# First stage of a graph and attention kernel: the load of x on two queues, roots and masks on GpSimd, the keys' first layer norm on ScalarE

## The chip, the cores and the metric

The kernel runs on one core of a Trainium2 chip. The core has TensorE (PE, matmuls), VectorE (DVE), ScalarE (ACT), GpSimd (POOL) and SyncE (SP), which work in parallel, each through its own instructions in order, and meet only at semaphores; 16 DMA engines move data. The metric is the device time of one execution in microseconds, lower is better. A profile comes from one execution of its own.

## The reference

The input is a graph of 6250 nodes with 256 features each and 106250 edges. With `xn` the layer norm of `x`:

```python
x = x + gnn(xn, edges) + mixer(xn)   # mixer: 4 layers of linear attention and feed-forward
x = x + experts(_layernorm(x))       # one of 32 experts for each node
# gnn: sums edge_attr by src with segment_sum, two dense layers
# mixer layer: h = layernorm(x, ln1_g, ln1_b); q = softmax(h Wq) over features,
#   k = softmax(h Wk) over the nodes; x += attention; x += gelu(layernorm(x) W1 + b1) W2 + b2
```

Only the first stage matters here. It does three things: it sorts the edges by their node's *kind* (the tile in which the node lies, 50 kinds), so that the sums by node can be made tile by tile later; it computes mean and variance of every row of `x`, and from them two layer norms (the first, `xn`, and the norm of `xn`, with which layer 0 begins); and it computes keys and queries of layer 0 for all nodes.

## The kernel before

Nodes lie as 50 tiles of 125 rows (`P = 125`, `TILES = 50`), taken in 25 pairs, the `GROUPS`. All of `x` stays in SBUF in `res`. Each engine has a program of its own, written out by hand; the order in each program is the order of its work.

*Load.* `block_.sync` issues the source indices `src_i`, then `res` in two halves of 25 tiles (3125 KB each, semaphores `X_LOADED[0]` and `[1]`), then the small vectors (`colrows`), then the mixer's weights.

*Sort.* VectorE makes, for each of 50 kinds, a 0/1 mask of 125x850 edges (`kind_mask`), and TensorE counts with it (`count_edges`). `first_ranks` turns the counts into starts. Then come the ranks: for kind `b`, TensorE computes with the mask the position of each edge (`rank_edges`, two halves in two banks), and VectorE writes it where the mask holds (`kind_place`, two predicated copies) and makes the mask of kind `b + 4`, as four mask buffers rotate. Eight kinds are placed ahead of the moments (`RANKS_EARLY = 8`); the other 42 go two to a key step, up to step 20.

*Statistics.* `moments` runs `bn_stats` on each tile, `variance` combines them, and `newton` computes the inverse root with 11 small operations, once for the first norm (`xst`) and once for the second (`kst`).

*Key phase.* 25 key steps, `key_step(t)` on each engine. VectorE: the shift by the maximum (`ek`), `key_normalise` (`xh`), the second placement of the step before, running maximum (`kmax`), softmax of the queries (`qstat`, `qd`, `qn`), the first placement of this step. TensorE: keys and queries of the pair before (`wqk`, 16 products), the first ranks, four transposes of `xh`, the weighing of an older pair (`xh,ek`), the second ranks. ScalarE: exponentials, a copy of the keys (`kr`), the scaled transposes (`h`), and the normalised `res`. GpSimd sums exponentials (`es`) and is otherwise free. Every fourth step or so computes a block's maximum (`MAX_AT`), the one behind it a block's sum (`SUM_AT`). When all kinds are placed, the positions go to the DMAs that scatter the edges; these run through the next three layers, on GpSimd.

TensorE transposes the small vectors (line 2125) after its early ranks, and ScalarE copies them to `cols`, which both it and VectorE await before the key phase.

## Time and profile before

| | us |
|---|---|
| median of 3 runs | 3080.54 |
| lowest, highest | 3072.39, 3084.48 |
| the profiled execution's own time | 3077.36 |
| its span in the profile | 3075.2 |

| engine | busy us | share of the span |
|---|---|---|
| TensorE, matmul | 2715.3 | 88% |
| VectorE | 2125.2 | 69% |
| GpSimd | 1723.8 | 56% |
| ScalarE | 1528.0 | 50% |

Line numbers (L1175) are those of the kernel before. A releaser behind an arrow is what the engine waited for. A matmul's end is modelled, so a group's time can overlap the next one's start. `PEclk` is the share of full speed that TensorE was granted, 0.50 or 1.00 at any moment, and a mean over a stretch. The DMA share is the mean over the 16 DMA engines.

### The profile page before, as it was taken

Reading aid. Unit: us, or ns where it says so; the run is one execution under the profiler, and the core shown is the slowest. Engines: PE = TensorE matmul, PEld = TensorE weight load, DVE = VectorE, ACT = ScalarE, POOL = GpSimd, SP = SyncE. Lnnn points to the kernel's source line nnn. Section 1 sums busy time; section 2 is a strip of 40 time slices with the busy share of each in tenths; the row PEclk is TensorE's granted clock in tenths of the full one; section 3 lists DMA queues with packets and bytes.
Section 4 is the critical chain, followed back from the end, with each engine's and each line's share of the span. In section 5 each row is a group of like instructions: output and inputs, shape, how many; then the busy total and the mean of one; then the engine's idle time right before and its main releaser. Section 6 shows DMA issues by size and latency. Waiting matters only on the chain.

```text
span 3075.2 us, 56118 instructions
## 1 busy us (share of the span) xinstructions
PE 2715.3 (88%) x18842; PEld 2482.9 (81%) x18842; DVE 2125.2 (69%) x4836; ACT 1528.0 (50%) x2947; POOL 1723.8 (56%) x1611
## 2 busy tenths in 40 slices
PE   4888899999979999997999999788888888992597
PEld 2666799999978999996889999688888888992465
DVE  8887567677756666675567767688888886893144
ACT  0333366666635566662565666344444445771254
POOL 0011178777758888885888885154454553224455
PEclk7898899999989999998999999799999998996688
DMA  3000223323232223223223221233323322201332
GB/s 119 24 27 25 82 50 68 68 61 64 54 93 66 63 68 65 59 62 95 64 59 68 65 64 43 64 108 84 87 81 87 82 81 60 59 25 50 85 100 76
DMA packets 255488, 207.87 MB, mean 68 GB/s; under 512 B 165433, under 2 KB 194314, under 8 KB 255205
## 3 DMA queue, kind: packets, MB, share of 16 engines
q1 hardware_dynamic: 197606, 162.55, 19.7%
q0 software_dynamic: 57600, 41.75, 7.0%
q8 instruction: 154, 2.52, 0.4%
q14 instruction: 128, 1.05, 0.1%
HBM read 136.93 MB, written 70.16 MB: 67 GB/s over the span
## 4 chain that ended last, share of the span: by engine, by line
PE 18%; POOL 13%; issue 8%; DVE 7%; DMA 4%; ACT 2%; DVEq 1%; SPq 0%; POOLq 0%; ACTq 0%
PE bank L375 16%; POOL edges_sorted L725 8%; DMA nodes_out<-orow,oidx 3%; POOL tokens_sorted L790 2%; DVE xh L1266 2%; PE bank L1808 1%; DVE hidh_lo L1302 1%; DMA staging<-in_edge_attr 1%; POOL r L703 1%; DVE oh L1494 1%; POOL ehl L742 1%; DVE bn L1257 1%; ACT hidh_hi L837 1%; ACT ehl L913 1%; ACT hid L831 0%
## 5 line engine op out<-in xcount | busy, mean ns | idle before, releaser
L725 POOL DMA_INDIRECT edges_sorted<-staging,pos_i x850 | 1058.2, 1245 | 254.2 <-issue 230.8
L831 ACT ACTIVATE hid<-bank,b1p 128x250 f32<-128x250 f32 x800 | 331.9, 466 | 388.0 <-PE bank L375 385.8
L375 PE MATMUL bank<-h_hi,w_hi 128*128 128x250 f32 x1600 | 482.7, 302 | 19.7 <-DVE h_lo L1286 19.7
L1302 DVE TENSOR_TENSOR hidh_lo<-hid,hidh_hi 128x500 fp32r<-128x500 f32 x400 | 296.9, 742 | 272.6 <-ACT hidh_hi L837 265.1
L375 PE MATMUL bank<-w_hi,hidh_hi 128*125 128x256 f32 x1600 | 468.1, 293 | 0.0
L375 PE MATMUL bank<-h_hi,w_lo 128*128 128x250 f32 x1600 | 451.1, 282 | 0.0
L375 PE MATMUL bank<-w_hi,hidh_lo 128*125 128x256 f32 x1600 | 450.9, 282 | 0.0
L375 PE MATMUL bank<-w_lo,hidh_hi 128*125 128x256 f32 x1600 | 449.8, 281 | 0.0
L375 PE MATMUL bank<-h_lo,w_hi 128*128 128x250 f32 x1600 | 448.0, 280 | 0.0
L375 PE MATMUL bank<-wqk,h 128*125 128x256 f32 x1600 | 380.6, 392 | 0.6 <-ACT mbc L882 0.6
L375 PEld LDWEIGHTS bank<-wqk,h 128*125 128x125 f32 x1600 | 306.3, 195 | 47.4 <-issue 1.2
L375 PEld LDWEIGHTS bank<-h_hi,w_hi 128*128 128x128 f32 x1600 | 307.0, 192 | 28.0 <-DVE h_lo L1286 24.2
L837 ACT CAST hidh_hi<-hid 128x500 fp32r<-128x500 f32 x400 | 243.8, 609 | 145.9 <-PE bank L375 139.6
L375 PEld LDWEIGHTS bank<-h_lo,w_hi 128*128 128x128 f32 x1600 | 308.4, 193 | 1.9
L375 PEld LDWEIGHTS bank<-h_hi,w_lo 128*128 128x128 f32 x1600 | 305.0, 191 | 0.0
L375 PEld LDWEIGHTS bank<-w_hi,hidh_hi 128*125 128x125 f32 x1600 | 298.6, 187 | 2.0
L375 PEld LDWEIGHTS bank<-w_lo,hidh_hi 128*125 128x125 f32 x1600 | 297.8, 186 | 2.2
L375 PEld LDWEIGHTS bank<-w_hi,hidh_lo 128*125 128x125 f32 x1600 | 297.3, 186 | 0.0
L703 POOL TENSOR_TENSOR r<-ve,minus_half 125x2 f32<-125x2 f32 x175 | 140.6, 804 | 271.5 <-DVE ve L1262 268.3
L1494 DVE TENSOR_TENSOR oh<-iota_node,kb 128x1000 fp32r<-128x1000 f32 x153 | 228.8, 1496 | 59.6 <-POOL kb L737 59.6
L1266 DVE TENSOR_SCALAR xh<-res,mv,r 125x256 f32<-125x256 f32 x350 | 159.0, 496 | 155.7 <-POOL r L703 155.7
L375 PE MATMUL bank<-ehl,oh 128*125 128x130 f32 x1224 | 164.4, 278 | 65.0 <-DVE agg L1482 65.0
(289 smaller groups left out, 5754.5 us busy)
## 6 DMA issues: line engine op xcount, KB each, us to landing
staging<-edges_sorted SPq DMA_DIRECT2D x103, 260.0 KB, 2.7
staging<-in_edge_attr SPq DMA_DIRECT2D x50, 531.2 KB
queries<-qn SPq DMA_DIRECT2D x100, 250.0 KB
qin<-queries SPq DMA_DIRECT2D x100, 250.0 KB
edges_sorted<-staging,pos_i POOLq DMA_INDIRECT x850, 3.7
rows_in<-edges_sorted SPq DMA_DIRECT2D x50, 260.0 KB, 2.7
yin<-tokens_sorted SPq DMA_DIRECT2D x81, 127.0 KB
raw<-in_L_mix_W SPq DMA_DIRECT2D x8, 1024.0 KB, 6.3
```

What stands on the lines that cost most here:

```text
L375: return nc.tensor.matmul(o, left, right, start=start, stop=stop, skip_group_check=True)
L703: nc.gpsimd.tensor_tensor(o[:, :], ve[:, :], minus_half[:, :], ALU.pow).then_inc(done, 1)
L725: nc.gpsimd.indirect_dma_start(out=edges_sorted, out_offset=bass.IndirectOffsetOnAxis(ap=pos_i[:, i:i + 1], axis=0), in_=stage[:, slot, j, ...
L742: nc.gpsimd.tensor_tensor(ehl[n % 4][:, :, EA + 2:2 * EA + 2], rows_in[n % RIN][:, :, 0:EA], f32(ehl[n % 4][:, :, 0:EA]), ALU.subtract).th ...
L790: nc.gpsimd.indirect_dma_start(out=tokens_sorted, out_offset=bass.IndirectOffsetOnAxis(ap=fpos_i[:, t:t + 1], axis=0), in_=res[:, t, :], i ...
L831: a = nc.scalar.activation(hid[c % 2][:, j, :], chunks(PH[c % 2])[:, j, :], ACT.Gelu, bias=b1p[:, 2 * c + j:2 * c + j + 1])
L837: nc.scalar.copy(hidh[c % 2][0][:, :, :], hid[c % 2][:, :, :]).then_inc(f_hi, 1)
L913: nc.scalar.copy(ehl[n % 4][:, :, 0:EA], rows_in[n % RIN][:, :, 0:EA]).then_inc(s_hi, 1)
L1257: step_(nc.vector.bn_stats(st[:, j, :], res_row(PAIR * g + j)))
L1266: a = nc.vector.tensor_scalar(o[:, j, :], res_row(PAIR * g + j), mv[:, j, 0:1], r[:, j:j + 1], ALU.subtract, ALU.mult)
L1302: nc.vector.tensor_tensor(hidh[c % 2][1][:, :, :], hid[c % 2][:, :, :], f32(hidh[c % 2][0][:, :, :]), ALU.subtract).then_inc(f_lo, 1)
L1494: nc.vector.tensor_tensor(oh[n % 4][:, :, :], iota_node[:, :].unsqueeze(1).to_broadcast((128, SEGR, P)), kb[:, n % 4, :].unsqueeze(2).to_b ...
```

## The change

- The second half of `x` is issued by ScalarE instead of SyncE, as ScalarE's first instruction.
- The two roots are powers (exponent -0.5) on GpSimd over 125x50; VectorE hands over the variance, and waits for the result. `newton` is gone.
- The early ranks move behind the moments, in two halves of four, each beside one of GpSimd's roots.
- The masks of kinds 12 to 49 are made by GpSimd, two a step from step 1 on, one step ahead of their use; VectorE no longer makes any in the key phase.
- The keys' first layer norm (`xh` of layer 0) is made by ScalarE, at the start of each key step.

```diff
-RSQRT_MAGIC = float(0x5f3759df)
+FIRST_ROOT = 2
...
+        def load_rows_of_x(eng, i):
+            w = slice(i * XPIECE, (i + 1) * XPIECE)
+            eng.dma_start(res[:, w, 0:D], x_rows[:, w, :]).then_inc(X_LOADED[i], 16)
...
-            for i in range(TILES // XPIECE):
-                w = slice(i * XPIECE, (i + 1) * XPIECE)
-                sp.dma_start(res[:, w, 0:D], x_rows[:, w, :]).then_inc(X_LOADED[i], 16)
+            load_rows_of_x(sp, 0)
...
+            for o, v, ready in ((xst[:, :, 0], lnt_x[:, 5, :], 1), (lnt_x[:, 6, :], lnt_x[:, 7, :], 2)):
+                pool.wait_ge(ln_stats, ready)
+                own_step(nc.gpsimd.tensor_tensor(o, v, minus_half[:, 0:1].to_broadcast((P, TILES)), ALU.pow))
...
+            def kind_mask(b):
+
+                if b == RANKS_EARLY + MASKS:
+                    pool.wait_ge(e_mask, SELECTORS + KINDS + b)
+                pool.wait_ge(e_acc, 2 * (b - MASKS + 1))
+                nc.gpsimd.tensor_scalar(kmask[(KINDS + b) % MASKS][:, :], kind16[:, :], float(b), None, ALU.is_equal).then_inc(e_mask, 1)
...
+                if l < 0:
+                    for b in RANKS_AT[t + 1] if 1 <= t < LAST else ():
+                        kind_mask(b)
...
+            load_rows_of_x(act, 1)
             act.wait_ge(consts, NCONST)
...
+            def first_normalise(g):
+                if g == 0:
+                    act.wait_ge(ln_stats, 3)
+                if g >= XR:
+                    act.wait_ge(g_prod, g - XR + 1)
+                    act.wait_ge(k_xT, g - XR + 1)
+                for j in range(PAIR):
+                    t = PAIR * g + j
+                    a = ident_act(xh2[g % XR][:, j, :], res_row(t), scale=kst[:, t, 0:1], bias=kst[:, t, 1:2])
+                a.then_inc(k_xh, 1)
...
             def key_step(t):
 
+                first_normalise(t)
                 if t >= 2:
                     exp_queries(0, t - 2)
...
-            for b in range(RANKS_EARLY):
-                kind_place(b)
-                kind_mask(KINDS + MASKS + b)
+
+            def early_ranks(first, end):
+                for b in range(first, end):
+                    kind_place(b)
+                    kind_mask(KINDS + MASKS + b)
 
             for t in range(TILES):
                 if t % XPIECE == 0:
                     dve.wait_ge(X_LOADED[t // XPIECE], 16)
                 moments(bn_x, t)
             variance(bn_x, lnt_x)
-            newton(lnt_x[:, 5, :], xst[:, :, 0], lnt_x, lnt_xi)
-            step_(shift(xst, lnt_x))
-
+            early_ranks(0, RANKS_EARLY // 2)
+
+            dve.wait_ge(p_step, FIRST_ROOT)
...
+            step_(shift(xst, lnt_x))
+            early_ranks(RANKS_EARLY // 2, RANKS_EARLY)
+            dve.wait_ge(p_step, FIRST_ROOT + 1)
+            step_(nc.vector.tensor_tensor(kst[:, :, 0], lnt_x[:, 6, :], xst[:, :, 0], ALU.mult))
...
                 for b in RANKS_AT[t][turn:turn + 1]:
                     kind_place(b)
-                    if MASKS + b < KINDS:
-                        kind_mask(KINDS + MASKS + b)
...
-                key_normalise(0, t)
```

VectorE between the early ranks and the first root, before (`kmask` is a mask, `staging<-kmask,bank` a placement, `bn_x` the moments, `lnt_x` the small statistics):

```order
L1175 COPY_PREDICATED staging<-kmask,bank 125x425 x2
L1169 TENSOR_SCALAR kmask<-kind 125x850
L1096 BN_STATS bn_x<-res 125x6 x50
L1111 TENSOR_TENSOR lnt_x<-bn_x 125x50
L1112 TENSOR_TENSOR lnt_x<-bn_x 125x50
```

and now, from the last operation of the first ranks on:

```order
L1215 TENSOR_TENSOR column<-staging,scr 50x850
L1124 BN_STATS bn_x<-res 125x6 x50
L1140 TENSOR_TENSOR lnt_x<-bn_x 125x50
L1141 TENSOR_TENSOR lnt_x<-bn_x 125x50
L1142 TENSOR_TENSOR lnt_x<-bn_x 125x50
L1144 TENSOR_TENSOR lnt_x<-lnt_x 125x50
L1146 SCALAR_TENSOR_TENSOR lnt_x<-lnt_x 125x50
L1148 TENSOR_SCALAR lnt_x<-lnt_x 125x50
L1186 COPY_PREDICATED staging<-kmask,bank 125x425 x2
L1180 TENSOR_SCALAR kmask<-kind 125x850
```

The 50 moments stand ahead of all placements now, where eight placements and masks stood ahead of them.

VectorE in one key step, before, from the first placement on (`ek` is the shift by the maximum, `xh_0` the key normalisation of a pair):

```order
L1175 COPY_PREDICATED staging<-kmask,bank 125x425 x2
L1169 TENSOR_SCALAR kmask<-kind 125x850
L1373 TENSOR_TENSOR ek<-kr,mbc 125x512
L1322 TENSOR_SCALAR xh_0<-res,kst 125x256 x2
L1175 COPY_PREDICATED staging<-kmask,bank 125x425 x2
L1169 TENSOR_SCALAR kmask<-kind 125x850
L1337 TENSOR_TENSOR kmax<-kmax,kr 125x512
L1418 TENSOR_REDUCE qstat<-qd 125x16
L1420 RECIPROCAL qstat<-qstat 125x16
L1424 TENSOR_TENSOR qn<-qd,qstat 125x512
L1407 TENSOR_REDUCE qstat<-bank 125x16
L1411 TENSOR_TENSOR qd<-bank,qstat 125x512
```

and now:

```order
L1186 COPY_PREDICATED staging<-kmask,bank 125x425 x2
L1381 TENSOR_TENSOR ek<-kr,mbc 125x512
L1186 COPY_PREDICATED staging<-kmask,bank 125x425 x2
L1345 TENSOR_TENSOR kmax<-kmax,kr 125x512
L1426 TENSOR_REDUCE qstat<-qd 125x16
L1428 RECIPROCAL qstat<-qstat 125x16
L1432 TENSOR_TENSOR qn<-qd,qstat 125x512
L1415 TENSOR_REDUCE qstat<-bank 125x16
L1419 TENSOR_TENSOR qd<-bank,qstat 125x512
```

Two masks and the pair's normalisation are gone from VectorE's step.

ScalarE from its start, before (`cols` are the small vectors):

```order
L813 ACT_TABLE_LOAD
L813 COPY cols<-bank 128x69
L809 ACTIVATE h<-bank,cols 128x250 x2
L809 ACTIVATE res<-res,xst 125x256 x2
L868 COPY kr<-bank 125x512
```

and now:

```order
L499 DMA res<-in_x 125x25x256
L830 ACT_TABLE_LOAD
L830 COPY cols<-bank 128x69
L825 ACTIVATE xh_0<-res,kst 125x256 x2
L825 ACTIVATE h<-bank,cols 128x250 x2
L825 ACTIVATE res<-res,xst 125x256 x2
L825 ACTIVATE xh_1<-res,kst 125x256 x2
L895 COPY kr<-bank 125x512
```

The second half of the load leads ScalarE's program, and the normalised pair for TensorE's transposes follows the table load and the copy of `cols`.

## Rows read from the trace of the kernel before

**Rows 1.** The page, part 1: busy us (share of the span) xinstructions, by engine.
```profile
PE 2715.3 (88%) x18842; PEld 2482.9 (81%) x18842; DVE 2125.2 (69%) x4836; ACT 1528.0 (50%) x2947; POOL 1723.8 (56%) x1611
```

**Rows 2.** Busy time by stretch (us); then PEclk granted, DMA share, GB/s.
```profile
7.00:34.00 27.00, 20.55 (x100) 14.19 (x100) 24.73 (x62) 0.00 (x0) 0.00 (x0) 1.00 0.34 117
34.00:57.00 23.00, 13.17 (x34) 5.40 (x34) 20.30 (x42) 0.00 (x0) 0.00 (x0) 0.61 0.34 116
60.00:65.00 5.00, 0.00 (x0) 0.00 (x0) 3.42 (x11) 0.00 (x0) 0.00 (x0) 0.50 0.93 241
...
200.00:250.00 50.00, 41.91 (x194) 33.50 (x192) 39.85 (x86) 18.62 (x37) 5.04 (x5) 0.90 0.08 23
```

**Rows 3.** The timeline, SyncE's DMA issues: start us, us, what.
```profile
1.25 27.36 SPq L517 DMA_DIRECT2D res<-in_x  x2
```

**Rows 4.** The timeline, VectorE, 0 to 75 us: start us, us, line, what.
```profile
6.59 0.60 DVE L1215 CAST src_f<-src_i 125x850 f32<-125x850 int32 x1 [1.53 <-DMA src_i<-in_src]
...
38.71 1.04 DVE L1204 TENSOR_TENSOR column<-staging,scr 50x850 bf16<-50x850 f32 x1
...
42.64 1.34 DVE L1175 COPY_PREDICATED staging<-kmask,bank 125x425 f32<-125x425 uint16 x2
...
44.40 1.34 DVE L1175 COPY_PREDICATED staging<-kmask,bank 125x425 f32<-125x425 uint16 x2
...
54.59 8.26 DVE L1096 BATCH_NORM_STATS2 bn_x<-res 125x6 f32<-125x256 f32 x25
64.42 8.26 DVE L1096 BATCH_NORM_STATS2 bn_x<-res 125x6 f32<-125x256 f32 x25 [1.58 <-DMA res<-in_x]
72.72 0.25 DVE L1111 TENSOR_TENSOR lnt_x<-bn_x 125x50 f32<-125x50 f32 x1
...
74.03 0.19 DVE L1124 TENSOR_SCALAR lnt_xi<-lnt_x 125x50 int32<-125x50 int32 x1
```

**Rows 5.** The timeline, TensorE and ScalarE, 65 to 82 us.
```profile
65.61 0.38 PE L2125 MATMUL bank<-ident,hid 69*128 69x69 f32 x1 [12.17 <-DMA hid<-in_L_gnn_u]
...
66.07 1.28 ACT L813 ACT_TABLE_LOAD   x1 [66.07 <-PE bank L2125]
...
67.36 0.22 ACT L813 COPY cols<-bank 128x69 f32<-128x69 f32 x1
...
81.47 1.09 PE L1808 MATMUL bank<-ident,xh 125*128 125x125 f32 x4 [14.07 <-DVE xh L1322]
```

**Rows 6.** Busy time of a normal key step.
```profile
216.00:224.00 8.00, 8.00 (x44) 6.82 (x43) 7.83 (x16) 3.61 (x7) 1.27 (x1) 1.00 0.11 34
```

**Rows 7.** Waits of TensorE, 81 to 350 us: total us, times, longest.
```profile
PE bank L375 <- DVE staging L1175: 21.2, 12, 2.9
```

**Rows 8.** The timeline, TensorE, 262 to 271 us.
```profile
262.82 0.34 PE L375 MATMUL bank<-kmask,tri 125*125 125x425 bf16 x1
...
269.95 0.59 PE L1808 MATMUL bank<-ident,xh 125*128 125x125 f32 x4
```

**Rows 9.** Groups by line, 81 to 350 us: busy us, mean ns.
```profile
L809 ACT ACTIVATE res<-res,xst 125x256 f32<-125x256 f32 x50 | 27.1, 592 | 0.0
...
L1322 DVE TENSOR_SCALAR xh<-res,kst 125x256 f32<-125x256 f32 x50 | 18.3, 408 | 0.0
...
L1169 DVE TENSOR_SCALAR kmask<-kind 125x850 bf16<-125x850 bf16 x38 | 16.0, 422 | 1.3
```

**Rows 10.** The timeline, GpSimd and VectorE, 286 to 289 us.
```profile
286.95 0.61 POOL L507 COPY es<-ek 125x512 f32<-125x512 f32 x1 [18.35 <-PE bank L375]
...
287.70 1.26 POOL L510 TENSOR_TENSOR es<-es,ek 125x512 f32<-125x512 f32 x1
287.94 1.31 DVE L1334 COPY kmax<-kr 125x512 f32<-125x512 f32 x1
```

**Rows 11.** One line's instructions: ns min/median/max, first and last start us.
```profile
L703 POOL TENSOR_TENSOR r<-ve,minus_half x175: 688/733/1261, 341.7 to 2518.9; 125x2 f32<-125x2 f32 x175
...
L1334 DVE COPY kmax<-kr x5: 419/420/420, 94.0 to 245.7; 125x512 f32<-125x512 f32 x5
```

More of the change, by code:

```diff
@@ L200, in build @@
         lnt_x = sb("lnt_x", [P, 8, TILES], F32, first_use)
-        lnt_xi = sb("lnt_xi", [P, TILES], I32, first_use)
         scr = [sb(f"scr{i}", [P, ECOL], F32, first_use) for i in range(3)]
@@ L814, in _ @@
             act.wait_ge(cols_ready, 1)
+            def first_normalise(g):
[8 more added lines that the diff above has]
+                a.then_inc(k_xh, 1)
             def normalise_input(g):
-                act.wait_ge(ln_stats, 1)
                 act.wait_ge(k_xh, g + 1)
@@ L1118, in variance @@
                 stepped()
-                step_(nc.vector.tensor_scalar(var, var_sum, 1.0 / D, EPS, ALU.mult, ALU.add))
-            def newton(v, o, w, wi):
-                stepped()
-                step_(nc.vector.tensor_scalar(wi[:, :], v.bitcast(I32), 1, None, ALU.logical_shift_right))
-                stepped()
-                y = w[:, 6, :]
-                step_(nc.vector.tensor_scalar(y.bitcast(I32), wi[:, :], -1.0, RSQRT_MAGIC, ALU.mult, ALU.add))
-                for r in range(3):
-                    vy, h, y_next = w[:, 1, :], w[:, 2, :], (w[:, 7, :], w[:, 6, :], o)[r]
-                    stepped()
-                    step_(nc.vector.tensor_tensor(vy, v, y, ALU.mult))
-                    stepped()
-                    step_(nc.vector.scalar_tensor_tensor(out=h, in0=vy, scalar=-0.5, in1=y, op0=ALU.mult, op1=ALU.mult))
-                    stepped()
-                    step_(nc.vector.scalar_tensor_tensor(out=y_next, in0=h, scalar=1.5, in1=y, op0=ALU.add, op1=ALU.mult))
-                    y = y_next
-                stepped()
+                nc.vector.tensor_scalar(var, var_sum, 1.0 / D, EPS, ALU.mult, ALU.add).then_inc(ln_stats, 1)
             def shift(o, w):
@@ L1245, in _ @@
             stepped()
-            step_(nc.vector.tensor_scalar(lnt_x[:, 5, :], lnt_x[:, 4, :], EPS, None, ALU.add))
-            newton(lnt_x[:, 5, :], lnt_x[:, 3, :], lnt_x, lnt_xi)
-            step_(nc.vector.tensor_tensor(kst[:, :, 0], lnt_x[:, 3, :], xst[:, :, 0], ALU.mult))
+            nc.vector.tensor_scalar(lnt_x[:, 7, :], lnt_x[:, 4, :], EPS, None, ALU.add).then_inc(ln_stats, 1)
+            step_(shift(xst, lnt_x))
+            early_ranks(RANKS_EARLY // 2, RANKS_EARLY)
+            dve.wait_ge(p_step, FIRST_ROOT + 1)
+            step_(nc.vector.tensor_tensor(kst[:, :, 0], lnt_x[:, 6, :], xst[:, :, 0], ALU.mult))
             stepped()
             shift(kst, lnt_x).then_inc(ln_stats, 1)
-            dve.wait_ge(ln_stats, 1)
             dve.wait_ge(cols_ready, 1)
@@ L1318, in key_normalise @@
                 o = xh2[m % XR]
-                if l == 0:
-                    for j in range(PAIR):
-                        t = PAIR * g + j
-                        a = nc.vector.tensor_scalar(o[:, j, :], res_row(t), kst[:, t, 0:1], kst[:, t, 1:2], ALU.mult, ALU.add)
-                else:
-                    dve.wait_ge(f_root, nth(l - 1, g) + 1)
-                    a = normalise(o, g, mv2, r2)
-                a.then_inc(k_xh, 1)
+                dve.wait_ge(f_root, nth(l - 1, g) + 1)
+                normalise(o, g, mv2, r2).then_inc(k_xh, 1)
             max_seen = [0]
```

## The prediction

> **What bounds the kernel now.** I read the page first: TensorE is busy 88% of the span, VectorE 69% [rows 1]. That is a mean over stages, and the change touches only the first of them, so I went on to the timeline of each engine from 0 to 85 us, the busy time by stretch, and the waits from 81 to 350 us.
>
> Up to 81.47 us TensorE does little; the first transposes of the key phase start there, after 14.07 us of idling that VectorE's xh ends [rows 5]. VectorE is the stage's chain. It sorts (first ranks done at 39.75), places the eight early kinds (a pair of placements and a mask every 1.76 us), and starts the moments of x at 54.59, 25 tiles in 8.26 us; the second 25 wait 1.58 us for their load and start at 64.42. Variance and the first root follow from 72.72 [rows 4]. The loads never idle: from 7 to 34 and from 34 to 57 us the DMA share is 0.34 at 117 and 116 GB/s, but from 60 to 65, when the mixer weights move, 0.93 at 241 GB/s [rows 2]. SyncE has issued both halves of x by 28.6 us [rows 3].
>
> In the key phase (25 steps, about 81 to 310 us) TensorE and VectorE hand work to each other. In a normal step both are full: 8.00 and 7.83 of 8 us [rows 6]. TensorE's own work of such a step is 7.13 us (first rank product at 262.82 to the next step's transposes at 269.95, a stretch that holds one step's products) [rows 8]. TensorE waits 21.2 us in all for placements, 12 times [rows 7].
>
> **x over two queues.** What would decide is whether the plateau belongs to SyncE's queue or to the DMA engines. The queue is not at its limit, since it moves 241 GB/s at share 0.93 three microseconds later [rows 2]; 0.34 of 16 engines is 5.4 engines, without a dip, for 50 us. So the limit goes with this kind of transfer (125 rows), and the second queue carries the same kind. Ends of the range: the second queue adds nothing, or it doubles the rate. I take nothing added. Then 2 x 3125 KB (3.2 MB each) at 116 GB/s take 55.2 us after the source indices (6.59 [rows 4]), to 61.8; the trace's own restart at 64.42 shows a tail of up to 2.6, so both halves land at about 63.1. The total is as before, but the *first* half, done by about 34 before (6.59 + 27.6), is now shared with the second and lands at 63 too. The indices share as well and may land a few us later; this hides behind the 23 us in which VectorE now waits.
>
> The Trainium skill, "DMA: Bandwidth & Descriptors", section "Why a DMA increments its semaphore by 16 and not by 1", has a rule against this edit: a transfer uses the largest number of engines up to 16 that divides its slowest dimension, the lowest-numbered ones, and 125 gives 5. Its section "Issuing engines are not separate DMA queues" adds that both queues run on the same engines. By that rule both halves land at 63; with other engines for the second queue they would land at about 36. The 5.4 engines of the trace agree with the five; nothing here has yet shown two queues at once.
>
> **The order on VectorE.** The moments now come *before* the early ranks. They start when the first half lands:
> - moments: 63.1 + 2 x 8.26 = 79.6; variance 72.72 to 74.03, 1.3 -> 80.9 [rows 4];
> - four early ranks, 4 x 1.76 = 7.0 -> 87.9; three small operations and a shift, 0.24 each (six stand between 72.72 and 74.03), 0.9 -> 88.8; four more ranks -> 95.9; two last operations 0.5 -> 96.4.
> The 22 operations of the two Newton roots, of 28 small ones between 74.03 [rows 4] and the first key normalisation's end just before 81.47 [rows 5], are gone. GpSimd's powers take their place: 2 columns take 0.73 us [rows 11] and here there are 50. Ends: 0.8 us if the cost is fixed, 18 us if it grows by column (0.73 x 50/2). I take 1 to 2, near the row of a 512-column addition (1.26) [rows 10]; the 7.0 us of ranks behind each root hide it, and beyond 7.0 each microsecond of a root counts.
>
> **TensorE and ScalarE at the handover.** TensorE transposes the vectors of constants after the last early rank. Before this was at 65.61, ahead of need. Now the last pair of products follows the seventh placement: 94.1 + 1.1 = 95.2, the transpose 0.4 -> 95.6, and ScalarE's table load and copy (66.07 to 67.58, 1.5) -> 97.2 [rows 5]. They were hidden and no longer are. Only then does ScalarE normalise the first pair: 2 x 0.54 = 1.1 (its res rows, 27.1 us for 50) [rows 9] -> 98.3, and the transposes start at 98.4. Against 81.47 that is **+16.9**. The same transposes took 1.09 us at 81.47 and 0.59 later [rows 5, 8], the lower and the upper level of TensorE's clock (the grant is 0.50 at 60 to 65 [rows 2]); early ranks now run just ahead, so some of the first step may be at full clock. Ends 0 and -3; I take **-1.5**.
>
> **The key phase.** VectorE loses 38 masks (16.0 us) and 50 key normalisations (18.3) [rows 9], 1.4 us a step. TensorE's 7.13 limits what comes through: 8.00 - 7.13 = 0.87 in each of about eight normal steps, **-7.0**. In the ten steps with a block's maximum or sum, and the one behind each, the wait starts at TensorE's own transposes and runs through maxima, softmax and placement; no mask or normalisation lies in it: 0. The first few steps have no slack that rows bound better; they stay in the range. Ends: 0, if GpSimd gives it back (below), and -28 (7 plus all 21.2 of the waits [rows 7]). ScalarE takes 25 x 1.1 us more where it is busy 18.62 of 50 us [rows 2], in front of an exponential that has a few tenths of slack. GpSimd's masks have a step's lead over TensorE. Each: 0.
>
> **Sum:** 16.9 - 1.5 - 7.0 = **+8.4 us**. The profiled execution took 3077.36; 3085.8. The median of the runs is 3.2 higher (3080.54), so I forecast **3089**. Later stages start on the same handshakes and shift one for one.
>
> **Rivals.**
> *Slower: GpSimd's masks hold VectorE.* When GpSimd's addition ran from 287.70 to 288.96, VectorE's copy beside it took 1.31 us instead of 0.42: held for 0.9 [rows 10, 11]. There are now two masks a step, each released at the end of a placement, just when VectorE goes on to an operation of that sort. A mask of 850 columns costs between 1.0 us (a copy's 0.61 for 512 columns, scaled) and 2.1 (the addition's 1.26, scaled) [rows 10]. If a mask is still running when VectorE reaches such an operation, which is so for both of a step from about 1 us of length on, each costs 0.9: 1.8 a step, more than the 1.4 won, so the -7 is gone, and in the ten block and sum steps 0.9 each lands on the chain, +9. Sum +24.4: **3105**. Against it: from 200 to 250 us GpSimd ran five such operations, and VectorE's steps beside them [rows 2, 6] show no such gap. The Trainium skill, "GPSIMD Engine Reference", section "Key points", says the two engines contend for SBUF where VectorE reads two SBUF inputs or runs in its two-port mode; the row agrees.
> *Faster: the two queues add.* Both halves at about 36. VectorE runs on from 39.75: moments to 56.3, variance 57.6, ranks and small work 15.5 -> 73.1, handover 2.0 -> 75.1: -6.4 against 81.47, and -7.0: **3067**. For it: nothing in the rows shows two queues at once. Against it: the plateau at 5.4 engines.
> *VectorE was the true bound.* All 34.3 us of its relief come through, with no clock gain: 16.9 - 34.3 = -17.4, **3063**. Against it: TensorE's 7.13 of 8.00.
>
> **Chances.** Forecast 0.65, GpSimd holds VectorE 0.15, queues add 0.13, VectorE the bound 0.07. A measurement of this kernel tells about 0.5% (15.4 us) from no change: 3065 to 3096. The forecast's own range is 3080 to 3096 (start 13 to 17, key phase -2 to -14, clock). The queues case straddles 3065, half on either side. Faster 0.10, same 0.71, slower 0.19. The range for 8 in 10 reaches to the queues case and nearly to the GpSimd case: 3066 to 3104.
>
> **What the profile would show.** DMA share still near 0.34 and 116 GB/s until about 61 us, VectorE idle from 40 to about 62, moments at about 63, first transposes at about 98, ScalarE's table load just before them. In the key phase a normal step near 7.1 to 7.5 us and VectorE busy some 6.5 of it. I am wrong if the share is near 0.68 at the start, if moments start at about 40, if a root takes over 7 us, or if VectorE's maxima and query products grow beyond 0.7 us.

## The result

| | before | after |
|---|---|---|
| median of 6 runs, us | 3081.07 | 3103.92 |
| lowest, highest | 3072.39, 3084.48 | 3099.59, 3108.93 |
| ratio, 95% interval | | 1.0079 [1.0065, 1.0094] |
| span of the profiled execution | 3075.2 | 3102.4 |

The kernel became slower by 0.8%, 22.9 us between the medians. The profiled execution of before lies some 4 us under its median, so the two traces differ by a little more, 27.2 us. The page of after, part 1, beside [rows 1]:

```profile
PE 2705.5 (87%) x18842; PEld 2478.0 (80%) x18842; DVE 2089.9 (67%) x4726; ACT 1545.9 (50%) x2997; POOL 1854.5 (60%) x1651
```

VectorE has 35 us less to do, GpSimd 131 more, and neither sets the time by its sum. To see where the time went, take two instructions that repeat through the program: the copy of the keys on ScalarE (`kr`, 25 times, the key phase) and GpSimd's small root (`r`, 175 times, layers 0 to 3). One tile's instructions, in before and then in after; the two numbers behind the comma are the first and the last start:

```profile
L868 ACT COPY kr<-bank x25: 586/586/587, 87.4 to 312.5; 125x512 f32<-125x512 f32 x25
```
```profile
L895 ACT COPY kr<-bank x25: 562/586/587, 108.0 to 324.6; 125x512 f32<-125x512 f32 x25
L709 POOL TENSOR_TENSOR r<-ve,minus_half x175: 695/737/1293, 352.2 to 2549.1; 125x2 f32<-125x2 f32 x175
```

With the root's row of before (341.7 to 2518.9, [rows 11]) the difference falls into five stretches:

| stretch | before | after | difference |
|---|---|---|---|
| start to first `kr` | 87.4 | 108.0 | +20.6 |
| first to last `kr` (key phase) | 225.1 | 216.6 | -8.5 |
| last `kr` to first root | 29.2 | 27.6 | -1.6 |
| first to last root (layers) | 2177.2 | 2196.9 | +19.7 |
| last root to the end | 556.3 | 553.3 | -3.0 |

The first three are the change's own, and near the forecast's +16.9 and -7. The fourth was forecast as nothing. Each kernel has one trace, and executions of one kernel on one chip lie up to 16 us apart, so a microsecond or two between two traces shows little.

**The start.** Busy time by stretch in after (PE, PEld, DVE, ACT, POOL; PEclk, DMA share, GB/s), beside [rows 2]:

```profile
7.00:34.00 27.00, 21.09 (x100) 14.54 (x100) 22.48 (x58) 0.00 (x0) 0.00 (x0) 1.00 0.34 118
34.00:57.00 23.00, 2.20 (x7) 1.01 (x6) 7.71 (x14) 0.00 (x0) 0.00 (x0) 0.62 0.34 119
```

The share of 0.34 is the same and the rate hardly differs from that with one queue. The timelines of VectorE, GpSimd, ScalarE and TensorE at the handover (start us, us, engine, line, what, and in brackets the idle time before it with its releaser):

```profile
65.13 16.45 DVE L1124 BATCH_NORM_STATS2 bn_x<-res 125x6 f32<-125x256 f32 x50 [22.51 <-DMA res<-in_x]
...
91.37 0.21 DVE L1255 SCALAR_TENSOR_TENSOR lnt_x<-lnt_x,xst 125x50 f32<-125x50 f32 x1 [1.72 <-POOL xst L705]
...
100.48 0.21 DVE L1263 TENSOR_TENSOR kst<-lnt_x,xst 125x50 f32<-125x50 f32 x1 [1.66 <-POOL lnt_x L705]
```
```profile
82.97 8.36 POOL L705 TENSOR_TENSOR xst<-lnt_x,minus_half 125x50 f32<-125x50 f32 x1 [77.44 <-DVE lnt_x L1148]
92.13 8.32 POOL L705 TENSOR_TENSOR lnt_x<-lnt_x,minus_half 125x50 f32<-125x50 f32 x1 [0.79 <-DVE lnt_x L1259]
```
```profile
97.93 1.28 ACT L830 ACT_TABLE_LOAD   x1 [97.93 <-PE bank L2130]
99.22 0.22 ACT L830 COPY cols<-bank 128x69 f32<-128x69 f32 x1
101.04 1.09 ACT L825 ACTIVATE xh<-res,kst 125x256 f32<-125x256 f32 x2 [1.60 <-DVE kst L1151]
```
```profile
102.19 1.10 PE L1813 MATMUL bank<-ident,xh 125*128 125x125 f32 x4 [2.70 <-ACT xh L825]
```

VectorE idles 22.51 us for a load whose halves now land together, at 65.1, where the first half was there by 39 (its moments start at 39.18 in the one-queue run below). Each root takes 8.3 us and is longer than the 7 us of ranks placed beside it. And the first transposes, 102.19 here against 81.47 [rows 5], start at VectorE's `kst`, the last thing that waits for the second root.

**The key phase.** TensorE's transposes of a pair, in normal steps, on the timeline, in before and then in after:

```profile
216.35 0.59 PE L1808 MATMUL bank<-ident,xh 125*128 125x125 f32 x4
223.42 0.59 PE L1808 MATMUL bank<-ident,xh 125*128 125x125 f32 x4
230.85 0.59 PE L1808 MATMUL bank<-ident,xh 125*128 125x125 f32 x4
```
```profile
155.60 0.59 PE L1813 MATMUL bank<-ident,xh 125*128 125x125 f32 x4
162.68 0.59 PE L1813 MATMUL bank<-ident,xh 125*128 125x125 f32 x4
169.75 0.59 PE L1813 MATMUL bank<-ident,xh 125*128 125x125 f32 x4
```

A normal step takes 7.07 us in after, TensorE's own work, as [rows 8] gave it (7.13). But before had such steps too: the one from 216.35 to 223.42 lies inside the window of [rows 6], whose 8.00 us are the width of the window and not the length of a step. From one copy of the keys to the next, the 24 steps of the phase gained this much:

| steps (from one `kr` to the next) | before | after | difference |
|---|---|---|---|
| the first four | 27.7 | 26.4 | -1.3 |
| nine normal ones | 66.2 | 64.1 | -2.2 |
| ten long ones (over 10 us, around a block's maximum or sum) | 125.6 | 120.4 | -5.2 |
| the last but one | 5.6 | 5.8 | +0.2 |

GpSimd's masks, by one tile's instructions (ns min/median/max, first and last start):

```profile
L722 POOL TENSOR_SCALAR kmask<-kind x38: 2328/2336/2931, 102.2 to 269.6; 125x850 bf16<-125x850 bf16 x38
```

**The layers.** GpSimd's scatters of edges in before and in after (groups of the page: busy us, mean ns, idle before them):

```profile
L725 POOL DMA_INDIRECT edges_sorted<-staging,pos_i x850 | 1058.2, 1245 | 254.2 <-issue 230.8
```
```profile
L738 POOL DMA_INDIRECT edges_sorted<-staging,pos_i x850 | 1083.1, 1274 | 255.1 <-issue 232.8
```

The same 850 instructions, which start from 402 to 1925 us, long behind the last mask (269.6), are 29 ns longer on the mean. The spread of a single one (ns min/median/max, first and last start), before and after:

```profile
L725 POOL DMA_INDIRECT edges_sorted<-staging,pos_i x850: 1172/1182/1776, 389.5 to 1893.9; - x170
```
```profile
L738 POOL DMA_INDIRECT edges_sorted<-staging,pos_i x850: 1182/1192/1746, 402.3 to 1924.8; - x170
```

So the usual scatter is only 10 ns longer. The rest of the 29 comes from the slow ones: 62 took more than 1.5 us in before, and 108 in after. GpSimd's roots stand between them, and VectorE's normalisation waits for the roots. VectorE's waits from 1000 to 2000 us (total us, times, longest), before and after:

```profile
DVE xh L1266 <- POOL r L703: 113.2, 55, 4.8
```
```profile
DVE xh L1280 <- POOL r L709: 136.0, 68, 4.8
```

### The profile page after: what moved, and what is told of

Read it like the earlier page. It is cut to its first block, busy times and chain, and to the rows that moved or that the text cites. A ratio compares the mean times of both kernels' runs of the same rounds, so it can differ in the third digit from the quotient of the medians.

```text
span 3102.4 us, 56074 instructions
## 1 busy us (share of the span) xinstructions
PE 2705.5 (87%) x18842; PEld 2478.0 (80%) x18842; DVE 2089.9 (67%) x4726; ACT 1545.9 (50%) x2997; POOL 1854.5 (60%) x1651
## 4 chain that ended last, share of the span: by engine, by line
PE 18%; POOL 14%; issue 8%; DVE 7%; DMA 3%; ACT 2%; DVEq 1%; POOLq 0%; ACTq 0%; SPq 0%
PE bank L374 16%; POOL edges_sorted L738 9%; DMA nodes_out<-orow,oidx 2%; POOL tokens_sorted L806 2%; DVE xh L1280 1%; DVE hidh_lo L1316 1%; PE bank L1813 1%; POOL r L709 1%; POOL ehl L755 1%; DVE oh L1502 1%; DVE bn L1271 1%; ACT ehl L940 1%; ACT hidh_hi L864 1%; PE bank L2258 0%; DVE res L1305 0%
## 5 line engine op out<-in xcount | busy, mean ns | idle before, releaser
L738 POOL DMA_INDIRECT edges_sorted<-staging,pos_i x850 | 1083.1, 1274 | 255.1 <-issue 232.8
L374 PE MATMUL bank<-h_hi,w_hi 128*128 128x250 f32 x1600 | 482.1, 301 | 19.8 <-DVE h_lo L1300 19.7
L755 POOL TENSOR_TENSOR ehl<-staging,ehl 128x512 fp32r<-128x512 f32 x103 | 130.3, 1265 | 161.2 <-ACT ehl L940 158.6
```

Source lines behind the costliest of these rows:

```text
L374: return nc.tensor.matmul(o, left, right, start=start, stop=stop, skip_group_check=True)
L738: nc.gpsimd.indirect_dma_start(out=edges_sorted, out_offset=bass.IndirectOffsetOnAxis(ap=pos_i[:, i:i + 1], axis=0), in_=stage[:, slot, j, ...
L755: nc.gpsimd.tensor_tensor(ehl[n % 4][:, :, EA + 2:2 * EA + 2], rows_in[n % RIN][:, :, 0:EA], f32(ehl[n % 4][:, :, 0:EA]), ALU.subtract).th ...
```

## The experiments

All ratios are against the kernel before on the same chip. Waits and counts that an edit brings with it (a load in two pieces is awaited at 32 instead of 16, `FIRST_ROOT` grows with the operations put ahead of it, e7 awaits `kst` twice more) are left out of the cuts below. The table holds what the sections below read; "scatter" is the mean of the 850 scatters in ns, "layers" the time from the first to the last small root.

| kernel | ratio [95%] | first `kr` | key phase | layers | scatter |
|---|---|---|---|---|---|
| before | | 87.4 | 225.1 | 2177.2 | 1245 |
| after | 1.0079 [1.0065, 1.0094] | 108.0 | 216.6 | 2196.9 | 1274 |
| e1_one_queue | 1.0056 [1.0036, 1.0076] | 99.3 | 216.7 | 2192.1 | 1270 |
| e2_queues_alone | 1.0045 [1.0028, 1.0062] | 96.0 | 225.0 | 2178.2 | 1244 |
| e3_wide_load | 1.0012 [1.0000, 1.0024] | 85.4 | 216.3 | 2191.2 | 1268 |
| e4_masks_back | 1.0063 [1.0044, 1.0081] | 108.2 | 217.6 | 2184.1 | 1251 |
| e5_wide_all | 0.9970 [0.9959, 0.9981] | 79.9 | 218.8 | 2180.3 | 1247 |
| e6_tiny_ops | 1.0091 [1.0076, 1.0106] | 108.1 | 216.8 | 2192.0 | 1269 |
| e7_norm_back | 1.0108 [1.0093, 1.0124] | 107.6 | 223.5 | 2191.1 | 1268 |
| e8_dead_masks | 1.0147 [1.0128, 1.0165] | 106.9 | 234.5 | 2190.2 | 1267 |
| e9_waits_only | 0.9971 [0.9959, 0.9982] | 80.6 | 220.2 | 2181.2 | 1245 |
| e10_ops_behind | 1.0017 [1.0007, 1.0026] | 80.6 | 220.3 | 2192.2 | 1267 |
| e11_ops_ahead | 1.0012 [1.0001, 1.0023] | 80.4 | 220.1 | 2192.8 | 1267 |
| e12_ahead_62 | 1.0009 [0.9997, 1.0021] | 80.4 | 220.1 | 2191.6 | 1269 |
| e13_other_kind | 0.9981 [0.9972, 0.9991] | 80.4 | 217.3 | 2182.6 | 1245 |
| e14_one_op | 0.9998 [0.9988, 1.0007] | 80.6 | 220.3 | 2192.8 | 1268 |

### The load: the queue or the shape

The theory is that the load is held by how many DMA engines its 125 rows occupy; the rival, that a queue is the limit. Three kernels: after with both halves on SyncE, before with the second half on ScalarE, and after with each half cut by partitions.

```diff
 # e1_one_queue, against after
             load_rows_of_x(sp, 0)
+            load_rows_of_x(sp, 1)
...
-            load_rows_of_x(act, 1)
```

> The changed kernel with both halves of x issued by SyncE again. Shared engines (my theory): the first half lands at about 34, the second at 64.4, so the moments of the first 25 tiles (8.2 us) hide, they end at about 72.8 instead of 81.6 and the first transposes come at about 93.5 instead of 102.2: 9 us less than the changed kernel, 3095, ratio to before 1.005. Rival, the second queue has engines of its own: x would land no earlier here and the time would stay at 3104. On the late loss (the changed kernel is 12.7 us late when layer 0 begins and 27 at the end): if ScalarE's queue causes it, it goes too and the time is about 3080; if not, it stays at some 14 us.

```diff
 # e2_queues_alone, against before: SyncE loads half 0, ScalarE half 1
+            act.dma_start(res[:, XPIECE:TILES, 0:D], x_rows[:, XPIECE:TILES, :]).then_inc(X_LOADED[1], 16)
             act.wait_ge(consts, NCONST)
```

> The kernel before with one edit: the second half of x is issued by ScalarE. Shared engines: both halves land at about 65, the moments start at 65.1 instead of 54.6 and end at 81.6 instead of 72.7, the rest is unchanged: +8.9, ratio 1.003. Rival, engines of its own: both land by 36 and the wait of 1.6 us goes: ratio 0.9995. If a second hardware queue also makes GpSimd's scatters slower (mean 1274 ns against 1245), the ratio is about 1.008.

```diff
 # e3_wide_load, against after
-            eng.dma_start(res[:, w, 0:D], x_rows[:, w, :]).then_inc(X_LOADED[i], 16)
+            for p in (slice(0, 112), slice(112, P)):
+                eng.dma_start(res[p, w, 0:D], x_rows[p, w, :]).then_inc(X_LOADED[i], 16)
```

> The changed kernel, each half of x loaded as 112 and 13 partitions instead of 125. If the load is bound by five of the sixteen engines, the DMA share rises from 0.34 to 0.9 or more, x lands before 35, the moments start when the first ranks end (about 42.6) and end at 59, the first transposes come at about 80 instead of 102: 22 us less than the changed kernel, 3082, ratio 1.000. If the memory or the queues bind, the share stays near 0.34 and the time at 3104.

The stretch from 15 to 25 us in e1, e2 and e3, in this order:

```profile
15.00:25.00 10.00, 10.00 (x57) 7.24 (x56) 10.00 (x28) 0.00 (x0) 0.00 (x0) 1.00 0.34 116
```
```profile
15.00:25.00 10.00, 10.00 (x51) 7.02 (x50) 8.86 (x26) 0.00 (x0) 0.00 (x0) 1.00 0.34 118
```
```profile
15.00:25.00 10.00, 10.00 (x53) 7.10 (x52) 9.16 (x26) 0.00 (x0) 0.00 (x0) 1.00 1.11 252
```

One queue or two, the share is 0.34 and the rate 116 to 118 GB/s. Cut into 112 and 13 rows, the same bytes through the same two queues go at 252 GB/s in this stretch. (The share adds up packet times, so it can pass 1 where packets overlap.) The Trainium skill's rule of the largest number up to 16 that divides the rows, in "DMA: Bandwidth & Descriptors", section "Why a DMA increments its semaphore by 16 and not by 1", gives 5 engines for 125 and 16 for 112; the shares agree with it. The rate doesn't last, and the load lands at 43.3, not before 35 as expected; VectorE waits 1.42 us for it (e3, from 25 to 30 us, and VectorE's moments):

```profile
25.00:30.00 5.00, 5.00 (x29) 3.61 (x28) 5.00 (x14) 0.00 (x0) 0.00 (x0) 1.00 1.10 141
```
```profile
43.32 16.44 DVE L1125 BATCH_NORM_STATS2 bn_x<-res 125x6 f32<-125x256 f32 x50 [1.42 <-DMA res<-in_x]
```

The moments in e1, whose second half lands at the time at which both land in after:

```profile
39.18 8.27 DVE L1124 BATCH_NORM_STATS2 bn_x<-res 125x6 f32<-125x256 f32 x25
...
64.44 8.27 DVE L1124 BATCH_NORM_STATS2 bn_x<-res 125x6 f32<-125x256 f32 x25 [16.98 <-DMA res<-in_x]
```

So the second queue gave nothing and took away the early half. That costs 8.7 us at the first `kr` (108.0 against 99.3 in e1) and in before 8.6 (96.0 against 87.4 in e2). The cut gives 22.6 in after, and with it the start is 2 us *ahead* of before. The queue rival falls.

With one queue (e1) the first `kr` is still 11.9 us later than before. Of these, 3.4 are what the roots exceed their cover. The other 8.5 are in the main the eight early ranks, which now stand behind the last moments: they take some 13.4 us, and the 22 Newton operations that went gave back 5.3 (0.24 each, an estimate). No run puts the ranks ahead of the moments again.

### The key phase: masks and norm

e4 gives the 38 masks back to VectorE, e7 gives it back the first norm, and e8 leaves VectorE its masks and has GpSimd make the same ones a second time, where nothing reads them.

```diff
 # e4_masks_back, against after: in VectorE's rank_step, and none in GpSimd's step
                     kind_place(b)
+                    if MASKS + b < KINDS:
+                        kind_mask(KINDS + MASKS + b)
```

> The changed kernel with the 38 masks of the key phase on VectorE again. Start as in the changed kernel (transposes at 102.2). If VectorE's relief is what shortens the steps, a normal step goes from 7.07 to about 7.6 us and layer 0 begins 4 us later, 3108. If GpSimd's masks (2.4 us each) hold VectorE, the step stays or shortens: 3100. If the late loss comes from masks on GpSimd, some 14 us of it go: 3094.

```diff
 # e7_norm_back, against after
             # ScalarE's key_step
-                first_normalise(t)
             # VectorE's key_step, with the loop of before in it
+                key_normalise(0, t)
```

> The changed kernel with the keys' first layer norm on VectorE again, masks on GpSimd. The masks' move alone gave 1.3 us of the 8 that the key phase won, so this run loses the other 6 to 7: key phase from the first transposes to the last key copy 229 us instead of 222.4, layer 0 at about 374; the late loss of 14 stays: 3110, ratio 1.010. If instead either move alone frees VectorE enough for TensorE's 7.1 us, the phase stays at 222 to 224 and the time at 3102.

```diff
 # e8_dead_masks, against e4, in GpSimd's key steps
+                        pool.wait_ge(p_step, own[0])
+                        pool.wait_ge(e_acc, 2 * (b - MASKS + 1))
+                        own_step(nc.gpsimd.tensor_scalar(stage[:, 1, :, :].rearrange("p c r -> p (c r)")[:, 0:ECOL // 2].bitcast(BF16), kind16[:, :], float(b), None, ALU.is_equal))
 # and on VectorE, in the step in which all kinds are placed
+                    dve.wait_ge(p_step, 41)
```

> Masks on VectorE, and GpSimd makes the same 38 masks of 850 columns too, into a place that nobody reads. Layer 0 at about 368 to 370. If GpSimd's wide 16-bit operations themselves leave the later scatters slower, their mean goes to about 1270 ns and the ratio to 1.010; if the cause is that the masks in use come from GpSimd (where the program's waits stand), it stays at 1251 and 1.0065.

The norm on ScalarE is worth 6.9 us (223.5 against 216.6), the masks on GpSimd 1.0 (217.6 against 216.6), which is hardly more than two traces can tell apart. The norm's gain isn't in the nine normal steps, which together take 0.6 us more in e7. It lies in the long ones; four of them, for one 12.94 us in e7 and 10.69 in after, make 6.4 of the 6.9. With the masks on VectorE (e4) normal steps already take TensorE's 7.07, so there the second relief had little left to win. What a mask on GpSimd costs VectorE depends on where it falls. VectorE and GpSimd in after, and then in e8, in a normal step:

```profile
157.44 0.68 DVE L1381 TENSOR_TENSOR ek<-kr,mbc 125x512 f32<-125x512 f32 x1
...
159.39 0.67 DVE L1345 TENSOR_TENSOR kmax<-kmax,kr 125x512 f32<-125x512 f32 x1
...
160.98 0.87 DVE L1432 TENSOR_TENSOR qn<-qd,qstat 125x512 f32<-125x512 f32 x1
...
157.64 5.10 POOL L722 TENSOR_SCALAR kmask<-kind 125x850 bf16<-125x850 bf16 x2 [0.64 <-DVE staging L1186]
```
```profile
159.50 1.38 DVE L1383 TENSOR_TENSOR ek<-kr,mbc 125x512 f32<-125x512 f32 x1
...
159.32 2.46 POOL L770 TENSOR_SCALAR staging<-kind 125x850 bf16<-125x850 bf16 x1 [1.40 <-DVE staging L1188]
```

In e8 VectorE's operation (`ek`, 512 columns) beside the mask takes 1.38 us instead of 0.68, and the key phase 16.9 us more than in e4: the slower rival's mechanism exists. Over the phase `ek` takes 1104 ns on the mean in e8 against 720 in e4, and `kmax` 1118 against 711. In after neither grew (713 and 714 ns, against 720 and 738 in before), though both overlap a mask in the lines above; only `qn` did, from 695 ns on the mean to 797, some 2.5 us in all. It isn't a matter of which began first: `ek` began ahead of the mask and `kmax` while it ran (the first of the two masks took 2.69 us, to 160.33), and neither was held. The visible differences that are left are the tensor that the mask writes and what VectorE ran just before; which one decides was not tried.

### The layers: what lengthens the scatters

e4 also brought the scatters back from 1274 to 1251 ns, and the layers from 2196.9 to 2184.1. So GpSimd's masks do harm long after the last of them. e6 kept the masks on VectorE and put an operation of two columns in the place of each on GpSimd.

```diff
 # e6_tiny_ops, against e4, in GpSimd's key steps
+                        pool.wait_ge(p_step, own[0])
+                        pool.wait_ge(e_acc, 2 * (b - MASKS + 1))
+                        own_step(nc.gpsimd.tensor_scalar(tot[:, 0:2], minus_half[:, :], float(b), None, ALU.is_equal))
```

> Masks on VectorE, and in the place of each of GpSimd's 38 masks an operation of 2 columns whose result nobody reads. Start and key phase as with the masks back (layer 0 at about 368). If the late loss comes from the number of instructions ahead of the scatters on GpSimd, the scatters' mean goes from 1251 to about 1270 ns and the ratio to 1.010; if it comes from the masks' own size or from what they hand over, it stays at 1251 and 1.006.

The scatters took 1269 ns: neither the masks' size nor their place on the path matters. Next, the best of the pieces became a base of its own: after with one queue, both loads cut, and the masks on VectorE.

```diff
 # e5_wide_all, against e4 with e1's and e3's edits
-            sp.dma_start(src_i[:, :], src.rearrange("(p c) -> p c", c=ECOL)).then_inc(src_loaded, 16)
+            for p in (slice(0, 112), slice(112, P)):
+                sp.dma_start(src_i[p, :], src.rearrange("(p c) -> p c", c=ECOL)[p, :]).then_inc(src_loaded, 16)
```

> What the first four runs point to, put together: the changed kernel with all of x and the source indices on SyncE's queue, each transfer cut into 112 and 13 partitions, and the masks of the key phase on VectorE. If the cut load was slowed only by what ran beside the indices (first ranks ended at 42.6 instead of 39.8), the indices land at about 3.5, the first ranks end at 37, the first transposes come at 74 (80.4 in the cut load), layer 0 begins at 340 and the late loss of 10 to 14 us is not there: 3062, ratio 0.9955. If the late loss is not from the masks on GpSimd but from an early start of the stages, it stays: about 3074, ratio 1.000.

It is faster than both kernels, 0.9970 of before. From it, four kernels separate waits, place and number. e9 has the 38 waits alone. e10 has the 38 small comparisons two a step in layer 3, behind all scatters; e11 has them in one piece ahead of the first root, and e12 has 62 there.

```diff
 # e9_waits_only, against e5, in GpSimd's key steps
+                        pool.wait_ge(e_acc, 2 * (b - MASKS + 1))
 # e10_ops_behind, against e5, in GpSimd's steps
+                if l == LAYERS - 1 and 1 <= t <= 19:
+                    for b in range(2):
+                        pool.wait_ge(p_step, own[0])
+                        own_step(nc.gpsimd.tensor_scalar(tot[:, 0:2], minus_half[:, :], float(b), None, ALU.is_equal))
 # e11_ops_ahead (38) and e12_ahead_62 (62), against e5, ahead of GpSimd's first root
+            for b in range(38):
+                pool.wait_ge(p_step, own[0])
+                own_step(nc.gpsimd.tensor_scalar(tot[:, 0:2], minus_half[:, :], float(b), None, ALU.is_equal))
```

> The fastest kernel so far (after, one queue, loads cut into 112 and 13 rows, masks on VectorE; 0.997 of before, scatters 1247 ns on the mean) with GpSimd's 38 waits on the rank products put back into its key steps, and nothing for them to guard. Theory 'waits': GpSimd's extra waiting is what lengthens the later scatters: mean 1267 to 1274 ns, and layers 1 and 2 take some 6 us more each, ratio about 1.002. Theory 'instructions': only instructions that stand ahead of the scatters count, and the waits ride on instructions that were there: scatters 1244 to 1251 ns, layers 1 and 2 as they were (552.7 and 553.1 us), ratio 0.997.

> The fastest kernel so far with 38 two-column operations on GpSimd placed in the steps of layer 3, behind all the scatters in its program. Theory 'position': only what stands ahead of the scatters lengthens them: scatters 1244 to 1251 ns, layers 1 and 2 at 552.7 and 553.1 us, ratio 0.997 to 0.998. Theory 'length': the length of GpSimd's program as a whole counts: scatters 1267 ns, layers 1 and 2 at 559 and 558, ratio about 1.002.

> The fastest kernel so far with the same 38 two-column operations in one piece ahead of the first root, while GpSimd would be idle, and none in the key phase. Theory 'position': as in the kernels with 38 instructions in the key phase, scatters 1267 to 1274 ns, layers 1 and 2 at 559 and 558 us, ratio about 1.001 to 1.003. Theory 'activity': what counts is that GpSimd works or waits in the key phase, beside VectorE and the others: scatters 1247 ns, layers 1 and 2 at 552.7 and 553.1, ratio 0.997.

> As the one before, with 62 operations ahead of the first root instead of 38. If 'position' means a number that grows with what stands ahead, scatters are at or above 1270 ns and the ratio at or above that of 38. If it means where the scatters come to lie in the program, in a pattern that repeats (62 and the two roots make 64 more instructions than before), scatters are back at 1244 to 1251 ns, layers 1 and 2 at 553 each, ratio 0.997. Theory 'activity': 1247 ns too, but then 38 ahead gave the same.

In e10 the last scatter starts before the first comparison does (first and last start, behind the comma):

```profile
L741 POOL DMA_INDIRECT edges_sorted<-staging,pos_i x850: 1182/1192/1748, 379.8 to 1896.5; - x170
```
```profile
L772 POOL TENSOR_SCALAR tot<-minus_half x38: 210/423/642, 2027.3 to 2429.2; 125x2 f32<-125x2 f32 x38
```

The waits do nothing (1245 ns), and the comparisons lengthen the scatters by the same 20 to 22 ns over e5 ahead of them, behind them, 38 or 62 of them. "Position" and "activity" both fall: an instruction that has not run yet can't have worked on anything. Left were the length of GpSimd's program, and one thing that all slow kernels share: they have a comparison with a constant (`tensor_scalar`) on GpSimd, and before, e2, e4, e5 and e9 have no instruction of that kind there (their `ident` and `tri` are made by another one, which the profile calls TENSOR_SCALAR_AFFINE_SELECT). The last pair tells these apart.

```diff
 # e13_other_kind, against e5, ahead of GpSimd's first root, 38 times
+                own_step(nc.gpsimd.tensor_tensor(tot[:, 0:2], minus_half[:, :], minus_half[:, :], ALU.subtract))
 # e14_one_op, against e5, ahead of GpSimd's first root, once
+                own_step(nc.gpsimd.tensor_scalar(tot[:, 0:2], minus_half[:, :], float(b), None, ALU.is_equal))
```

> The fastest kernel so far with 38 two-column operations ahead of GpSimd's first root, in the place where 38 comparisons with a constant (tensor_scalar) made the later scatters 1267 ns long. Here they are subtractions of two tensors, a kind of instruction that the kernel before has on GpSimd too. Theory 'length': any 38 instructions more in GpSimd's program do it: scatters 1267 ns on the mean, layers 1 and 2 at 559 and 557 us, ratio about 1.001. Theory 'kind': it is the comparison with a constant, of which GpSimd's program had none before: scatters 1244 to 1251 ns, layers 1 and 2 at 552.7 and 553.1 us, ratio 0.997.

> The fastest kernel so far with a single two-column comparison with a constant (tensor_scalar) ahead of GpSimd's first root. Theory 'kind': one instruction of this kind in the program is enough: scatters 1267 ns on the mean, layers 1 and 2 at 559 and 557 us, ratio about 1.001. Theory 'length': one instruction more changes nothing: scatters 1244 to 1251 ns, layers 1 and 2 at 552.7 and 553.1 us, ratio 0.997. Both runs fast would say that it takes many instructions of this kind, both slow that any added instruction does it.

The scatters, and VectorE's wait for the roots from 1000 to 2000 us, in e13 and then in e14:

```profile
L745 POOL DMA_INDIRECT edges_sorted<-staging,pos_i x850 | 1058.5, 1245 | 255.1 <-issue 232.8
...
DVE xh L1283 <- POOL r L716: 104.3, 53, 4.8
```
```profile
L745 POOL DMA_INDIRECT edges_sorted<-staging,pos_i x850 | 1077.7, 1268 | 255.6 <-issue 233.2
...
DVE xh L1283 <- POOL r L716: 134.3, 67, 4.9
```

The spread of a single scatter, and the small roots' first and last start, e13 and then e14:

```profile
L745 POOL DMA_INDIRECT edges_sorted<-staging,pos_i x850: 1172/1182/1730, 375.1 to 1880.5; - x170
L716 POOL TENSOR_TENSOR r<-ve,minus_half x175: 695/740/1267, 324.9 to 2507.5; 125x2 f32<-125x2 f32 x175
```
```profile
L745 POOL DMA_INDIRECT edges_sorted<-staging,pos_i x850: 1186/1192/2014, 378.1 to 1896.7; - x170
L716 POOL TENSOR_TENSOR r<-ve,minus_half x175: 697/742/1303, 327.9 to 2520.7; 125x2 f32<-125x2 f32 x175
```

38 subtractions: 1245 ns. **One** comparison of two columns, which ran at 5.8 us and took 0.54: 1268 ns, and the layers take 10.2 us more than in e13 (2192.8 against 2182.6). Timed, the ratio is 0.9998 against 0.9981 (5.9 us between the medians of ten runs each on one chip; e13's trace is of its fastest run, which widens the 10.2). On another chip, e10 to e12 lie 12.6 to 13.4 us above e9. All ten kernels with the instruction show the same in the scatters, a median of 1190 to 1192 ns and 89 to 108 of them above 1.5 us; the six without it have 1182 to 1185 ns and 59 to 68. The kind of instruction decides, and once is enough. Every `tensor_scalar` tried was a comparison (`is_equal`), so another operation in it stays untried.

## Why the prediction was wrong

Forecast: 3089, no change that can be measured. Measured: 3103.92, slower. That it lies inside the 8 in 10 range (to 3104) is luck, and so is its closeness to the slower rival's 3105, whose mechanism is not what happened. Between the two traces the difference is 27.2 us where the sum had 8.4: 5.2 of the excess are at the start, -3.1 in and just behind the key phase, and 16.7 come later. By its own steps:

- **x over two queues, nothing added: right.** Share 0.34 and 118 GB/s; e1, e2 and e3 show it from three sides. The landing was 2 us later than forecast (65.1 against 63.1), since I took the rate of the plateau and only part of the tail that the trace showed at 64.42 [rows 4].
- **The root on GpSimd, "1 to 2 us": mis-sized.** It measured 8.36 and 8.32 us. The row nearest in operation, 0.73 us for two columns [rows 11], bounded it at 18; I leaned on an addition instead, which is another operation. The cover of 7.0 us hid most of it; 1.72 and 1.66 us were left over, as "beyond 7.0 each microsecond of a root counts" says. A root over 7 us was one of its own signs of being wrong.
- **The handover, +16.9: measured +20.7** (102.19 against 81.47). The landing (2.0) and the two roots (3.4) make 5.4 more than forecast, and 1.6 of them came back: the ranks between were a little quicker, and ScalarE's table load was off the chain, since the second root, by way of `kst`, ended the wait last. The clock gain of 1.5 in the first step didn't come either: the first transposes took 1.10 us, as before.
- **The key phase, -7: near in size (-8.5), and by luck.** TensorE's 7.07 is indeed the floor of a normal step, and the placement waits stayed (19.7 us against 21.2). But "8.00 - 7.13 = 0.87 in each of about eight normal steps" took the width of a window for the length of a step; the nine normal steps gave 2.2 us. 5.2 came from the ten long steps, priced at 0 ("no mask or normalisation lies in it"), and 1.3 from the first four. The forecast didn't say which part earns it; e4 and e7 do: the norm nearly all, the masks next to nothing.
- **"GpSimd's masks hold VectorE": refuted here** but for the 2.5 us on `qn`, though its price is real, as e8 shows. A mask took 2.33 us at the least, above the upper end of 2.1 that I had scaled from an addition.
- **"Later stages start on the same handshakes and shift one for one": this step failed.** They took 16.7 us more (+19.7 and -3.0). GpSimd's scatters, which the change doesn't touch, became longer by 29 ns on the mean, and the roots between them were later for VectorE. Up to the first root of layer 0 the sum held to within 2.1 us (+10.5 against +8.4); what was priced at nothing is that an instruction on GpSimd changes how long GpSimd's other instructions take. The kernels with a `tensor_scalar` on GpSimd have layers 8 to 13 us longer than their pairs without (e6 and after against e4, e10 to e12 against e9, e14 against e13). The rest of the 19.7 is not settled: e4, e5, e9 and e13, without one, still have layers of 2180.3 to 2184.1 against 2177.2. All of them have the two large roots on GpSimd and the norm on ScalarE, which no run took away alone from them; a part can also be the difference between two executions.

Why one instruction of a kind lengthens others stays open. The runs show that it needn't have run yet, so it is something that comes with the program as a whole; none of them shows what.

In sum: 20.6 at the start, of which 8.7 is the second queue, 3.4 the roots and most of the rest the ranks behind the moments; -10.1 in and just behind the key phase; +16.7 later. With all loads on one queue and cut to 112 and 13 rows, and the masks left on VectorE (e5), the rest of the change is worth its work: 3062.23 us against 3071.20 on the same chip.

## What to carry to other kernels

Before a transfer gets a second queue, look at its DMA share: a flat 0.34 means few engines by its shape, and a cut of the partitions (112 and 13 instead of 125) doubled the rate for most of the load, where a second queue added nothing and delayed the half that was needed first. A window in which an engine is always busy gives no step's length: take that from one instruction's start to the same one's next. Move to another engine only what the *next* bound leaves room for; the masks' 16 us on VectorE were worth about 1. And an engine's first instruction of a new kind isn't free just because it is off the path: compare the durations of that engine's untouched instructions before and after.

## What the runs showed of the hardware

- One two-column `tensor_scalar` (a comparison) ahead in GpSimd's program made its 850 scatters 1268 ns long on the mean instead of 1245, and 38 of them behind the last scatter made them 1267; 38 subtractions of tensors did not.
- GpSimd took 8.3 us for a power over 125x50 and 0.73 us over 125x2, so its cost grows with the columns: 7.6 us more for 48 more, 0.16 us each between these two sizes.
- GpSimd compared 850 bf16 columns with a constant in 2.34 us at the median; VectorE's masks take 0.42 on the mean [rows 9].
- VectorE's `ek` (two tensors of 512 columns) took 1.38 us beside such a comparison in e8 and 0.68 in after, where `kmax` (two tensors as well) took 0.67.
- Halves of 3125 KB in 125 rows came at 116 to 119 GB/s over one queue or two, and in 112 and 13 rows at 252 from 15 to 25 us and at 219 from 7 to 34.
